# Seven of 39 expert slots cut from 256 rows to 128 in a mixture-of-experts layer

## The chip, the core and the metric

The kernel runs on one core of one Trainium2 chip. TensorE (PE) does the matrix products, VectorE (DVE) and ScalarE (ACT) the elementwise work, GpSimd (POOL) the indirect transfers, and SyncE (SP) issues the other transfers. The metric is the device time of one execution in microseconds (us): the median over several.

## The reference, cut to what matters

Two layers act on 4096 tokens of 256 numbers (x is 16 x 256 x 256). The change lies in the last part, the expert layer:

```python
shared = new_gelu(xf @ Wfc_s + bfc_s) @ Wproj_s + bproj_s
probs = softmax(xf @ Wr)                       # 8 experts
topk_p, topk_i = top_k(probs, 2); topk_p = topk_p / sum(topk_p)
gate[token, topk_i] += topk_p
for e in range(8):
    h = new_gelu(xf @ Wfc[e] + bfc[e]) @ Wproj[e] + bproj[e]     # 256 -> 1024 -> 256
    routed = routed + h * gate[:, e:e+1]
out = shared + routed
```

Each token needs two experts only, so 8192 rows (token, expert) are to be computed. How many fall to an expert is known only on the chip.

## The kernel before, in words

Attention, a quantised feed-forward layer and a Fourier stage come first and are not touched. The function `moe` normalises the tokens, runs the shared expert over 16 chunks of 256 tokens, and beside it VectorE works out the routing: `picks`, `slots_of_experts`, `slot_tables` (L2174: how many slots each expert takes, where they start, which expert each slot has), `row_ends` and `positions` (L2194: the place of each row). Then GpSimd sends each token's row to its two places in a table in memory, `slots_x`, by 64 indirect transfers (L1858).

The table is cut into slots of 256 rows; each slot belongs to one expert. An expert with n rows takes n/256 slots, rounded up, so at most (8192 + 8 x 255)/256 = 39 slots can be needed, and the program always works through 39; places without a token hold zeros and the number of no token. A slot is one round of `tick(s)`, which each engine runs in its own order:

- PE (L2049): `rows_T(s+1)` turns the next slot's rows (4 matmuls of 128x128, L1989); `first(s)` makes the hidden layer: 48 matmuls (8 column blocks x 2 halves of the input x 3 products of high and low parts), whose moving operand is the slot's 256 rows (L2004); `second(s-1)` makes the output of the slot before: for each 128 rows 24 matmuls whose moving operand is 256 weight columns (L2017).
- ACT: `copy_rows(s+1)` (L1912), `gelu(s)` (L1928).
- DVE: `low_rows(s+1)` (L2231), `shares(s+1)`, `cut(s)` into high and low half precision parts (L2135, L2137), `output(s-1)` (L2245, L2250).
- SP, one queue in this order: `slot_rows(s+2)` (L1812), `first_weights(s+2)` (L1797, 1 MB, waits for `gelu(s)`), `second_weights(s+1)` (L1804, 1 MB, waits until `output(s-1)` has read the products).
- POOL: `own` (L1864) and `add_rows` (L1872): two indirect transfers for each slot that add 128 rows each onto the result in memory; those of a slot start when those of the slot before have landed.

Weights, rows and results have two buffers each, by the parity of the slot. `walk` (L1748) writes ticks 0 and 1 out, loops 18 times over two ticks, and writes out the last. SP's and POOL's programs are written out in full.

Of the kernel before, what the change touches and what calls it, by code (L numbers as in the profile page):

```python
# [18 lines left out]
P = 128  # L19
# [1612 lines left out]

def moe(nc, d, g, X, ident, banks, halves_dram, out):
# [6 lines left out]
    NSLOT = (PICKS * NT * P + NE * (SLOT - 1)) // SLOT  # L1640
# [9 lines left out]
    with ExitStack() as ctx:  # L1650
# [6 lines left out]
        slots_x = nc.dram_tensor("slots_x", [NSLOT * SLOT, W], F32).ap()  # L1657
# [14 lines left out]
        e_table = sb("e_table", [P, NE, MOST])  # L1672
        s_table = sb("s_table", [P, NSLOT, NE])
# [12 lines left out]
        cmp_e = sb("cmp_e", [P, NE, MOST])  # L1686
        n_slots = sb("n_slots", [P, NE])
        start = sb("start", [P, NE + 1])
        cmp_s = sb("cmp_s", [P, NSLOT, NE])
        slot_ef = sb("slot_ef", [P, NSLOT])  # L1690
# [57 lines left out]
        def walk(eng, tick):  # L1748

            for s in range(2):  # L1750
                tick(s, s)
            with eng.Fori(1, NSLOT // 2) as i:
                for p in range(2):
                    tick(2 * i + p, p)
            for s in range(2 * (NSLOT // 2), NSLOT + 1):
                tick(s, s % 2)
# [5 lines left out]
        assert CHUNKS % 2 == 0 and NSLOT % 2 == 1  # L1762
# [11 lines left out]
        def _(sp):  # L1774
# [11 lines left out]
            n = NSLOT * SLOT // P  # L1786
# [3 lines left out]
            def expert(s):  # L1790
                return sp.value_load(slot_e[0:1, bass.ts(s, 1)], min_val=0, max_val=NE - 1)

            def first_weights(s, p):
                e = expert(s)
# [5 lines left out]
            def second_weights(s, p):  # L1800
                e = expert(s)
# [5 lines left out]
            def slot_rows(s, p):  # L1807
# [4 lines left out]
                sp.dma_start(rows[p][:], slots_x[bass.ts(s, SLOT), :].rearrange("(t p) c -> p t c", p=P)).then_inc(e_r[p], 16)  # L1812
# [12 lines left out]
            slot_rows(1, 1)  # L1825
            for c in range(CHUNKS - 4, CHUNKS):
                store_shared(c)
            first_weights(1, 1)
            second_weights(1, 1)

            def tick(s, p):
                if not (known(s) and s + 2 >= NSLOT):
                    slot_rows(s + 2, p)
                    first_weights(s + 2, p)
                if not (known(s) and (s < 1 or s + 1 >= NSLOT)):
                    second_weights(s + 1, 1 - p)

            for s in range(NSLOT + 1):
                tick(s, s % 2)

        @block.gpsimd
        def _(pool):
# [18 lines left out]
            def own(s):  # L1861
                p = s % 2
                pool.wait_ge(e_r[p], 8 * (s - p) + 16)
                pool.tensor_copy(owner[:, s, :], rows[p][:, :, TOKEN].bitcast(I32)).then_inc(e_own, 1)  # L1864

            def add_rows(s):
                pool.wait_ge(e_gt, s + 1)
                pool.wait_ge(e_own, s + 1)
                if s >= 1:
                    pool.wait_ge(e_sa, 16 * ST * s)  # L1870
                for t in range(ST):
# [11 lines left out]
            pool.wait_ge(e_sa, 16 * ST * NSLOT)  # L1883

        @block.scalar
        def _(act):
# [21 lines left out]
            def copy_rows(s, p):  # L1908
# [3 lines left out]
                act.activation(rT[p][:, 0, :, :].rearrange("p k t -> p (k t)"), banks[3][:, 512:1024], ACT.Copy).then_inc(e_rh, 1)  # L1912

            def gelu(n, p, buffer, ahead=()):
                ahead = list(ahead)
                for jp in range(J // 2):
# [8 lines left out]
                    for q in range(2):  # L1925
                        j = 2 * jp + q
                        src = banks[jp // 2][:, (jp % 2) * 512 + q * SLOT:(jp % 2) * 512 + (q + 1) * SLOT]
                        ins = act.activation(hf[p][:, j, :], src, ACT.Gelu_apprx_tanh, bias=b1[buffer][:, j:j + 1], scale=1.0 / WSCALE)  # L1928
# [22 lines left out]
            def tick(s, p):  # L1951
                if not (known(s) and s + 1 >= NSLOT):
                    copy_rows(s + 1, 1 - p)
# [424 lines left out]
```

## Time and profile before

| | us |
|---|---|
| median of 3 runs | 1328.8 (1327.67 to 1331.16) |
| the profiled execution | 1334.27 |
| its span, first to last instruction | 1332.5 |
| PE busy | 1170.6 (88%) |
| DVE busy | 851.9 (64%) |
| mean granted TensorE clock | 0.964 of full |

The span is read in stages: the shared expert from about 660 us to 870, the scatter of rows from 788 to 884, and the 39 slots from 887 to the end.

### The profile page before, as it was taken

What the parts mean: (1) busy time and instruction counts of PE and PEld (TensorE: products, weight loads), DVE (VectorE), ACT (ScalarE), POOL (GpSimd) and SP (SyncE); (2) the same over time, 40 slices, a digit from 0 to 9 for tenths busy, and PEclk for the clock granted to TensorE, in tenths of its full rate; (3) what the DMA queues carried; (4) which work ended last, traced back from release to release, by engine and by line L of the source; (5) the groups of instructions that cost most, each with busy time, mean ns of one, the idle gap of its engine ahead of it and who ended that gap; (6) DMA issues with size and microseconds to landing.
All of it is one profiled execution on the core that took longest, in us unless ns stands there. A gap on an engine that the chain in (4) does not pass through costs nothing. (4 is left out here: it accounts for less than half of the span.)

```text
span 1332.5 us, 28452 instructions
## 1 busy us (share of the span) xinstructions
PE 1170.6 (88%) x10152; PEld 891.3 (67%) x10152; DVE 851.9 (64%) x2620; ACT 595.4 (45%) x1065; POOL 587.4 (44%) x651
## 2 busy tenths in 40 slices
PE   0699999998678989975789999939999999999996
PEld 0144444444324668864679888828899999999995
DVE  3999999987796722255564785525666666666663
ACT  1388778777436612242075433313333333333331
POOL 6487787785610078952000026632333333333333
PEclk9999999999798999988979999969999999999999
DMA  9488879883500046502294043256888887888881
GB/s 277 86 169 167 173 170 168 176 184 103 190 2 1 1 142 213 181 32 73 82 262 102 1 164 107 99 177 213 256 253 252 252 252 241 248 250 247 252 256 50
DMA packets 183549, 217.30 MB, mean 163 GB/s; under 512 B 92944, under 2 KB 166288, under 8 KB 170912
## 3 DMA queue, kind: packets, MB, share of 16 engines
q1 hardware_dynamic: 169152, 199.19, 52.4%
q0 software_dynamic: 14304, 16.93, 6.1%
q8 instruction: 51, 0.84, 0.3%
q14 instruction: 42, 0.34, 0.1%
HBM read 144.70 MB, written 52.23 MB: 148 GB/s over the span
## 5 line engine op out<-in xcount | busy, mean ns | idle before, releaser
L2017 PE MATMUL banks<-moe_w,moe_hT 128*128 128x256 f16 x2640 | 296.9, 273 | 0.0
L2017 PEld LDWEIGHTS banks<-moe_w,moe_hT 128*128 128x128 f16 x2640 | 258.4, 98 | 30.0
L1928 ACT ACTIVATE moe_hf<-banks,moe_b 128x256 f32<-128x256 f32 x440 | 184.9, 471 | 171.0 <-PE banks L2004 171.0
L1872 POOL DMA_INDIRECT out_x<-moe_y,slot_owner x78 | 122.3, 1568 | 287.3 <-DVE moe_y L2250 238.2
L2004 PE MATMUL banks<-moe_rT,moe_w 128*128 128x256 f16 x1872 | 213.2, 274 | 0.0
L747 DVE CUSTOM_DVE_ANT_0 masked<-banks,mask_bias 128x256 f32<-128x256 f32 x512 | 185.9, 420 | 32.5 <-PE banks L569 28.6
L2004 PEld LDWEIGHTS banks<-moe_rT,moe_w 128*128 128x128 f16 x1872 | 184.6, 99 | 22.0
L2137 DVE TENSOR_TENSOR moe_hT<-moe_hf,moe_hT 128x512 f16<-128x512 f32 x220 | 153.9, 699 | 7.6
L479 ACT ACTIVATE probsT<-banks 128x1024 f32<-128x1024 f32 x128 | 130.7, 1021 | 50.4 <-PE banks L600 50.4
L569 PE MATMUL banks<-kT,qT 48*128 48x256 f16 x512 | 92.3, 285 | 50.8 <-DMA qT<-q_split 31.4
L1858 POOL DMA_INDIRECT slots_x<-moe_xn,pos x64 | 62.8, 981 | 155.1 <-DVE pos L2201 123.1
L2135 DVE CAST moe_hT<-moe_hf 128x512 f16<-128x512 f32 x220 | 95.4, 434 | 40.9 <-ACT moe_hf L1928 32.7
L1912 ACT ACTIVATE moe_rT<-banks 128x512 f16<-128x512 f32 x39 | 23.3, 597 | 209.8 <-PE banks L1989 209.8
L151 POOL TENSOR_SCALAR half_rows<-half_rows 128x512 f32<-128x512 f32 x72 | 108.1, 1502 | 10.9 <-issue 5.5
L2245 DVE SCALAR_TENSOR_TENSOR moe_y<-banks,moe_b 128x512 f32<-128x512 f32 x39 | 27.0, 692 | 133.5 <-PE banks L2017 133.5
L569 PEld LDWEIGHTS banks<-kT,qT 48*128 48x128 f16 x512 | 34.2, 95 | 108.7 <-issue 57.6
L2004 PE MATMUL banks<-moe_xnT,moe_w 128*128 128x256 f16 x768 | 91.3, 277 | 0.0
L155 POOL TENSOR_TENSOR half_parts<-half_rows,half_parts 128x512 f16<-128x512 f32 x72 | 84.8, 1178 | 6.2
L582 PE MATMUL banks<-qmT,kT 64*128 64x256 f16 x512 | 85.8, 278 | 0.0
L2004 PEld LDWEIGHTS banks<-moe_xnT,moe_w 128*128 128x128 f16 x768 | 76.4, 100 | 9.5
L1085 PE MATMUL banks<-xqT,w1T 128*128 128x512 bf16 x256 | 67.8, 395 | 12.5 <-ACT hf L1044 5.7
L615 PE MATMUL banks<-probsT,v_ones 128*32 128x256 f32 x1024 | 69.9, 392 | 0.3 <-ACT qmT L486 0.3
(322 smaller groups left out, 1783.4 us busy)
## 6 DMA issues: line engine op xcount, KB each, us to landing
moe_w<-moe_halves SPq DMA_DIRECT2D x80, 1024.0 KB, 5.0
moe_halves<-half_parts SPq DMA_DIRECT2D x18, 1024.0 KB, 6.1
slots_x<-empty_row SPq DMA_DIRECT2D x1, 10140.0 KB, 50.9
moe_rows<-slots_x SPq DMA_DIRECT2D x39, 260.0 KB, 5.9
half_rows<-in_L_ffn_Wfc SPq DMA_DIRECT2D x8, 1024.0 KB, 8.6
half_rows<-in_L_ffn_Wproj SPq DMA_DIRECT2D x8, 1024.0 KB, 8.5
moe_b<-in_L_ffn_bproj SPq DMA_DIRECT2D x39, 128.0 KB, 5.4
ctx_rows<-in_ctx SPq DMA_DIRECT2D x16, 256.0 KB, 3.0
```

Of the source, the lines that this page charges most:

```text
L151: pool.tensor_scalar(rows[:, cols], rows[:, cols], WSCALE, None, ALU.mult).then_inc(w["cut"], 1)
L155: pool.tensor_tensor(parts[:, 1, cols], rows[:, cols], parts[:, 0, cols], ALU.subtract).then_inc(w["cut"], 1)
L479: act.activation(probsT[n % EXPS][:].rearrange("p j k q -> p (j k q)"), psum_t[n % 2][:], ACT.Exp, scale=SCALE).then_inc(s_exp, 1)
L569: ins = pe.matmul(psum_s[:, at:at + S], qT[b % 2][rows, hp, t * P:(t + 1) * P], kT[b % 3][rows, hp, :], start=(t == 0), stop=(t == NQ - 1))
L582: pe.matmul(psum_t[n % 2][:, at:at + S], kT[b % 3][rows, hp, k * P:(k + 1) * P], qmT[b % 2][rows, hp, :], start=(k == 0), stop=False)
L747: ins = v.tensor_tensor_reduce(masked[2 * j + t][:], psum_s[:, at:at + S], mask_bias[b % 2][:, t, :], 1.0 / SHIFT, -3e38, ALU.add, ALU.max ...
L1872: pool.indirect_dma_start(out=out_rows, out_offset=bass.IndirectOffsetOnAxis(ap=owner[:, s, t:t + 1], axis=0), in_=y[s % 2][:, t, :], in_o ...
L1928: ins = act.activation(hf[p][:, j, :], src, ACT.Gelu_apprx_tanh, bias=b1[buffer][:, j:j + 1], scale=1.0 / WSCALE)
L2004: ins = pe.matmul(banks[jp // 2][:, at:at + SLOT], w1[buffer][:, w, k, j * P:(j + 1) * P], moving(x, k), start=(k == 0 and (w, x) == PARTS ...
L2017: ins = pe.matmul(OUT[p][:, t * D:(t + 1) * D], hT[p][:, x, j, t * P:(t + 1) * P], w2[buffer][:, w, j, :], start=(j == 0 and (w, x) == PAR ...
L2135: v.tensor_copy(hT[p][:, 0, at, :], hf[p][:, at, :]).then_inc(e_hh, 1)
L2137: v.tensor_tensor(hT[p][:, 1, at, :], hf[p][:, at, :], hT[p][:, 0, at, :], ALU.subtract).then_inc(e_hl, 1)
```

## The change

The 39 slots become 32 of 256 rows ("whole") and 7 of 128 ("half"). Rounds 2, 8, 14, 20, 26, 32 and 38 work on a half slot, the others on a whole one. In `slots_x` the whole slots lie first and the halves behind them, 71 tiles of 128 rows in place of 78. An expert's rows fill whole slots, and its last rows go to a half slot if there are at most 128 of them; if more whole slots are wanted than there are, a pair of halves is used as a whole one. So `slot_tables` counts both kinds, and `positions` moves the rows that lie in a half. `tick` takes the loop's number and the place in a period of six rounds; `walk` now writes out 6 ticks, loops 5 times over 6, and writes out the last 4.

```diff
+    halves = (2 * rows + NE * (SLOT - 2)) // SLOT
+    few = NE - 1
+    return (halves - few) // 2 + few, few, (halves - few) // 2
...
-            for s in range(2):
-                tick(s, s)
-            with eng.Fori(1, NSLOT // 2) as i:
-                for p in range(2):
-                    tick(2 * i + p, p)
+            for r in range(PERIOD):
+                tick(0, r)
+            with eng.Fori(1, NSLOT // PERIOD) as i:
+                for r in range(PERIOD):
+                    tick(i, r)
...
+        def tiles(r):
+            return 1 if r % PERIOD == HALF_AT else ST
...
-                for t in range(ST):
+                for t in range(tiles(s)):
                     pool.indirect_dma_start(out=out_rows, ...
...
-                ins = pe.matmul(banks[jp // 2][:, at:at + SLOT], w1[buffer][:, w, k, j * P:(j + 1) * P], moving(x, k),
+                ins = pe.matmul(banks[jp // 2][:, at:at + width], w1[buffer][:, w, k, j * P:(j + 1) * P], moving(x, k),
...
-                for t in range(ST):
+                for t in range(parts):
                     for j in range(J):
...
+                link(v.tensor_scalar(spill[:], start[:, NE, 0:1], -float(WHOLES), 0.0, ALU.add, ALU.max))
+                link(v.tensor_tensor(half_start[:], start[:, 0:NE, 1], start[:, 0:NE, 0], ALU.subtract))
...
+                link(v.tensor_tensor(tmp[:], base[:], over(whole_rows[:], full, 1), ALU.is_ge))
+                link(v.tensor_tensor(tmp[:], tmp[:], over(half_move[:], full, 1), ALU.mult))
                 link(v.scalar_tensor_tensor(base[:], over(start[:, 0:NE, 0], full, 1), float(SLOT), base[:], ALU.mult, ALU.add))
+                link(v.tensor_tensor(base[:], base[:], tmp[:], ALU.add))
```

On PE, in the last rounds of the program (behind the loop), the kernel before has the hidden layer of slot 38 and the outputs of slots 37 and 38; `moe_hT` is the hidden layer, `moe_w_0` and `moe_w_1` the weight buffers:

```order
L1752 COMPARE_AND_BRANCH
L2004 MATMUL banks<-moe_rT,moe_w_0 128x256 x48
L2017 MATMUL banks<-moe_w_1,moe_hT 128x256 x48
L2017 MATMUL banks<-moe_w_0,moe_hT 128x256 x48
L1650 UNCONDITIONAL_BRANCH
```

The changed kernel has slots 36, 37 and 38 there, of which 38 is a half:

```order
L1767 COMPARE_AND_BRANCH
L2027 MATMUL banks<-ident,moe_rows 128x128 x4
L2042 MATMUL banks<-moe_rT,moe_w_0 128x256 x48
L2055 MATMUL banks<-moe_w_1,moe_hT 128x256 x48
L2027 MATMUL banks<-ident,moe_rows 128x128 x2
L2042 MATMUL banks<-moe_rT,moe_w_1 128x256 x48
L2055 MATMUL banks<-moe_w_0,moe_hT 128x256 x48
L2042 MATMUL banks<-moe_rT,moe_w_0 128x128 x48
L2055 MATMUL banks<-moe_w_1,moe_hT 128x256 x48
L2055 MATMUL banks<-moe_w_0,moe_hT 128x256 x24
L1660 UNCONDITIONAL_BRANCH
```

A half slot keeps its 48 matmuls in the hidden layer, with 128 columns in place of 256, has 24 in place of 48 in the output, and 2 turns in place of 4. Its two weight transfers stay whole.

On VectorE the slot tables of the changed kernel read so; the names are those of the tables, `start` the running count of slots:

```order
L2218 TENSOR_TENSOR start<-start,n_slots 128x2 x8
L2219 TENSOR_SCALAR spill<-start 128x1
L2220 TENSOR_TENSOR half_start<-start 128x8
L2221 SCALAR_TENSOR_TENSOR half_start<-spill,half_start 128x8
L2222 TENSOR_TENSOR cmp_s<-s_table,start 128x312
L2223 TENSOR_TENSOR cmp_s<-s_table,half_start 128x56
L2224 TENSOR_REDUCE slot_ef<-cmp_s 128x46
L2225 SCALAR_TENSOR_TENSOR slot_ef<-cmp_s,slot_ef 128x7
L2226 TENSOR_TENSOR slot_ef<-slot_ef 128x7
L2227 TENSOR_SCALAR slot_rank<-slot_ef 128x39
L2228 TENSOR_SCALAR slot_e<-slot_ef 128x39
L2229 TENSOR_SCALAR whole_rows<-n_slots 128x8
```

Before, `start` was followed by one comparison, one sum and the two last conversions; the rest of these rows, and four more of 8 columns behind them, are new.

## Rows read from the trace of the kernel before

**Rows 1.** Page, the chain that ended last: share of the span
```profile
PE 38%; POOL 4%; DMA 3%; issue 2%; DVE 2%; SPq 0%; ACT 0%; POOLq 0%; DVEq 0%
```

**Rows 2.** Busy time by stretch: us, busy (instructions), PEclk, DMA share, GB/s
```profile
core 0: us, PE busy (x) PEld busy (x) DVE busy (x) ACT busy (x) POOL busy (x), PEclk, DMA share, GB/s
950.00:1300.00 350.00, 350.00 (x3209) 315.16 (x3207) 216.57 (x450) 127.16 (x290) 116.24 (x97) 1.00 0.83 251
```

**Rows 3.** Chain in order of time, one slot: start, us, what
```profile
1076.25 0.44 PE banks L1989 x4
1076.68 5.24 PE banks L2004 x48
1081.92 5.24 PE banks L2017 x48
```

**Rows 4.** Timeline of PE, 128-column matmuls with their own weights: start, us
```profile
338.54 1.07 PE L1060 MATMUL banks<-ident_bf,w1q_rounded 128*128 128x128 bf16 x16 [2.41 <-POOL pick_bias L988]
339.45 1.06 PE L1060 MATMUL banks<-ident_bf,w2q_rounded 128*128 128x128 bf16 x16
```

**Rows 5.** Timeline, end of the program
```profile
1316.01 0.69 DVE L2245 SCALAR_TENSOR_TENSOR moe_y<-banks,moe_b 128x512 f32<-128x512 f32 x1 [3.21 <-PE banks L2017]
...
1318.13 1.54 POOL L1872 DMA_INDIRECT out_x<-moe_y,slot_owner  x1 [6.54 <-DVE moe_y L2250]
...
1323.51 1.54 POOL L1872 DMA_INDIRECT out_x<-moe_y,slot_owner  x1 [1.99 <-DMA out_x<-moe_y,slot_owner]
1325.36 1.54 POOL L1872 DMA_INDIRECT out_x<-moe_y,slot_owner  x1 [0.30 <-issue]
```

**Rows 6.** Timeline, routing on VectorE and start of the scatter
```profile
772.40 1.52 DVE L2179 TENSOR_TENSOR start<-start,n_slots 128x1 f32<-128x1 f32 x8
...
775.30 0.42 DVE L2135 CAST moe_hT<-moe_hf 128x512 f16<-128x512 f32 x1
...
780.78 0.69 DVE L2142 SCALAR_TENSOR_TENSOR X<-banks,X 128x512 f32<-128x512 f32 x1 [1.15 <-PE banks L2017]
...
783.51 0.42 DVE L2195 TENSOR_TENSOR moe_base<-moe_base,tot 128x256 f32<-128x256 f32 x1
783.96 0.43 DVE L2196 TENSOR_TENSOR moe_base<-moe_base,moe_total 128x256 f32<-128x256 f32 x1
...
787.88 1.22 POOL L1858 DMA_INDIRECT slots_x<-moe_xn,pos  x1 [123.09 <-DVE pos L2201]
```

**Rows 7.** Timeline of SP's queue, one slot
```profile
1077.39 0.34 SPq L1804 DMA_DIRECT2D moe_w<-moe_halves  x1
1077.91 0.33 SPq L1805 DMA_DIRECT2D moe_b<-in_L_ffn_bproj  x1
1078.36 0.38 SPq L1812 DMA_DIRECT2D moe_rows<-slots_x  x1
1082.98 0.34 SPq L1797 DMA_DIRECT2D moe_w<-moe_halves  x1
```

**Rows 8.** The tile moe_rows: issue to landing
```profile
DMA to landing us min/median/max: 2.8/5.9/8.1
```

**Rows 9.** Busy time by stretch, around the end of a weight transfer
```profile
1087.50:1088.00 0.50, 0.50 (x7) 0.44 (x6) 0.50 (x1) 0.28 (x1) 0.00 (x0) 1.00 1.02 390
1088.50:1089.00 0.50, 0.50 (x7) 0.44 (x6) 0.50 (x3) 0.00 (x0) 0.00 (x0) 1.00 0.11 34
```

**Rows 10.** Timeline of PE, where the second slot starts
```profile
899.69 1.05 PE L1989 MATMUL banks<-ident,moe_rows 128*128 128x128 f32 x4 [2.52 <-DMA moe_rows<-slots_x]
```

**Rows 11.** Busy time by stretch, behind that wait
```profile
900.00:902.00 2.00, 2.00 (x11) 1.53 (x10) 0.59 (x1) 0.60 (x1) 0.00 (x0) 0.50 0.91 366
```

**Rows 12.** Chain in order of time, the hidden layer behind that wait
```profile
900.74 6.51 PE banks L2004 x48
```

**Rows 13.** Page, DMA queues: instruction packets of the whole program
```profile
q8 instruction: 51, 0.84, 0.3%
```

**Rows 14.** DMA queues from 950 to 1300 us: the only instruction packets
```profile
q14 instruction: 6, 0.05, 0.0%
```

More of the change, by code:

```diff
@@ L1748, in walk, with slot, tiles_before, place @@
         def walk(eng, tick):
-            for s in range(2):
-                tick(s, s)
-            with eng.Fori(1, NSLOT // 2) as i:
-                for p in range(2):
-                    tick(2 * i + p, p)
-            for s in range(2 * (NSLOT // 2), NSLOT + 1):
-                tick(s, s % 2)
+            for r in range(PERIOD):
[3 more added lines that the diff above has]
+                    tick(i, r)
+            for r in range(NSLOT % PERIOD + 1):
+                tick(NSLOT // PERIOD, r)
+        def slot(i, r):
+            return PERIOD * i + r
+        def tiles(r):
+            return 1 if r % PERIOD == HALF_AT else ST
+        def tiles_before(i, r):
+            whole, r = divmod(r, PERIOD)
+            return (ST * PERIOD - 1) * (i + whole) + sum(tiles(x) for x in range(r))
+        def place(i, r):
+            whole, r = divmod(r, PERIOD)
+            if r == HALF_AT:
+                return WHOLES + i + whole
+            return (PERIOD - 1) * (i + whole) + r - (r > HALF_AT)
+        def first_tile(i, r):
+            whole, q = divmod(r, PERIOD)
+            if q == HALF_AT:
+                return ST * WHOLES + i + whole
+            return ST * place(i, r)
         def known(s):
@@ L1798, in first_weights, with second_weights @@
                 sp.dma_start(b1[p][:], d["moe_b1"][bass.ds(e, 1)].rearrange("o p j -> p (o j)")).then_inc(e_w1[p], 16)
-            def second_weights(s, p):
-                e = expert(s)
+            def second_weights(i, r):
+                s, p, e = slot(i, r), r % 2, expert(i, r)
                 if not (known(s) and s == 0):
@@ L1824, in _ @@
             slot_rows(0, 0)
-            slot_rows(1, 1)
+            slot_rows(0, 1)
             for c in range(CHUNKS - 4, CHUNKS):
                 store_shared(c)
[L1828 to L1839, printed above, removed]
+            first_weights(0, 1)
+            second_weights(0, 1)
+            for s in range(NSLOT - 1):
+                if s + 2 < NSLOT:
+                    slot_rows(*divmod(s + 2, PERIOD))
+                    first_weights(*divmod(s + 2, PERIOD))
+                if s >= 1:
+                    second_weights(*divmod(s + 1, PERIOD))
         @block.gpsimd
@@ L2237, in shares @@
+            def shares(i, r):
+                s, p, n = slot(i, r), r % 2, tiles(r)
+                mine = share[:, bass.ds(ST * s, n)]
+                v.scalar_tensor_tensor(mine, rows[p][:, 0:n, RANK], slot_rank[:, bass.ts(place(i, r), 1)], rows[p][:, 0:n, EXTRA], ALU.is_equal, ALU.mult).then_inc(e_shr, 1)
                 v.wait_ge(e_shr, 2 * s + 1)
-                v.tensor_tensor(mine, mine, rows[p][:, :, GATE], ALU.add).then_inc(e_shr, 1)
-            def output(s, p):
+                v.tensor_tensor(mine, mine, rows[p][:, 0:n, GATE], ALU.add).then_inc(e_shr, 1)
@@ L2257, in tick @@
                 if not (known(s) and s >= NSLOT):
-                    cut(CHUNKS + s, p)
+                    cut(CHUNKS + s, p, width=tiles(r) * P)
                 if not (known(s) and s < 1):
-                    output(s - 1, 1 - p)
+                    output(i, r - 1)
             low_rows(0, 0)
@@ L2339, in routing_tables @@
     SLOT = 256
-    nslot = (2 * tokens + NE * (SLOT - 1)) // SLOT
+    nslot, halves, wholes = slot_counts(2 * tokens, NE)
+    full = np.arange(tokens // SLOT) * SLOT
+    both = np.concatenate([full + SLOT // 2, full])
+    order = np.concatenate([np.arange(wholes), wholes + np.arange(halves) // 2, np.arange(halves)])
     f = np.float32
```

152 lines of the change are left out of this document (88 added, 64 removed).

## The prediction

> **What bounds the kernel now.** I read first the page's chain of waits: PE holds 38% of what ended last, POOL 4% and the DMAs 3% [rows 1]. The rest of the chain is not named there, since it lies in stages that the change doesn't touch. Then the busy time by stretch: from 950 to 1300 us PE is busy for 350.00 of 350 us, at the full clock (2.4 GHz), while DVE has 217 us, ACT 127 and POOL 116, and the DMA engines are busy 0.83 of the time at 251 GB/s [rows 2]. So in the slots PE alone sets the time, and the DMA is the one other resource that is not far from its limit. The chain there is a plain repetition: 0.44 us of turns, 5.24 us of `first`, 5.24 us of `second`, 10.92 us for each slot of 256 rows [rows 3]. That is 109.2 ns for each matmul of 256 columns.
>
> **The change part by part.**
>
> *Hidden layer of a half slot.* 48 matmuls of 128 columns in place of 256. The trace has such matmuls elsewhere, each with weights of its own: 16 take 339.45 - 338.54 = 0.91 us from start to start, 57 ns each [rows 4]; a little of that is the group's first, so I take 56. Saved: 48 x (109.2 - 56) = 2.55 us for each half, 7 x 2.55 = 17.9 us.
>
> The Trainium skill ("TensorE: Matmul & The Clock Gate", Back-to-back issue gap) says that in a stream of weight loads and matmuls the spacing at 128 columns is about 81 ns, since both share the pipeline. By it the hidden layer of a half would give 48 x 28.2 = 1.35 us, 9.5 us in all. The 57 ns of the row are for just such pairs and speak against it; it is a rival below.
>
> *Output of a half slot.* 24 matmuls of 256 columns go: 24 x 109.2 = 2.62 us, 18.3 us for seven. *Turns.* 2 of 4 go, 0.22 us, 1.5 us for seven. PE's sum is 37.7 us.
>
> *The end.* The output of the last slot is on another path. The product of slot 37 is ready at 1316.0, its additions start at 1318.1, and those of slot 38 wait until they have landed at 1323.5 [rows 5]. That wait doesn't shrink with slot 38's 2.62 us on PE. What goes is the second of its two additions, 1325.36 - 1323.51 = 1.85 us. So 0.8 us of the sum is given back.
>
> *Routing on VectorE.* The slot tables get 11 more instructions on 1 to 56 columns, and three grow. The eight small ones of before take 1.55 us from start to start, 0.19 each [rows 6]; 11 x 0.2 is 2.2, and the wider ones add some 0.3: 2.5 us. Behind them stands the cutting of a chunk, which starts at 775.30; behind it DVE waits 1.15 us for PE, until 780.78 [rows 6]. So 1.15 us of the 2.5 is hidden and 1.35 is late. `positions` gets three instructions of 256 columns at 783.96 - 783.51 = 0.45 us [rows 6], 1.35 us, all in the open: the scatter waits for it and for nothing else (POOL idle for 123 us until `pos`). The scatter starts 2.7 us later, and so do the slots. PE doesn't feel it earlier: `second` of that chunk comes one `first` (5.24 us) behind 780.8, at 786, and its cut, which ended 1.15 us before 780.78, now ends at 782.1. Bounds: 1.35 us (if the tables were hidden) and 4 us.
>
> *First slots.* PE waits 2.52 us for the rows of slot 2 [rows 10]. They are a half slot now; half of their bytes (130 KB) at 251 GB/s are 0.5 us less.
>
> *Transfers.* Each half still wants 2 MB of weights and 128 KB of bias, against half of the rows and of the additions. Over six rounds the bytes fall from 16.5 to some 16.1 MB while PE's time falls from 65.5 to 60.1 us: 268 GB/s, against 251 at 0.83 busy, which would be 302 at 1.0. On average it fits. What is tight is one transfer: the rows of slot s+2. SP issues them behind `second_weights`, 2.1 us after the round's start at 1076.25 [rows 3, 7], they land 5.9 us later (median) [rows 8], at 8.0 us, and PE wants them at the start of the next round, at 10.92. The slack is 2.9 us. A round with the half slot's `first` takes 0.44 + 2.69 + 5.24 = 8.37 us, and the round behind it, with its `second`, 0.44 + 5.24 + 2.62 = 8.30. In the first the rows come about 0.3 us early. In the second the queue is still full: `first_weights` is issued 2.55 us earlier in the short round, but moves only behind the rows, from 7.5 us on. A weight transfer takes about 4 us (1 MB at 251 GB/s), so it ends near 11.5 to 12, while the next `second_weights` would begin to move at about 10.7; before, the queue had run empty at that point (390 GB/s, then 34) [rows 9]. So these rows land about 1.3 us later than usual, at 9.3 against 8.30: PE waits 1.0 us. For six halves (none follows the seventh): 6.0 us. Bounds: 0 if the transfers are fast enough to keep the order, and 2.5 us each if the additions in memory, which run beside them, slow the weights further: 0 to 15 us. I take 6.0. The new waits stand in front of the turns on PE, so `first` and `second` of that round move with them; the transfers issued after them move as well, which gives the queue the time to empty. The other rounds have 2.9 us to spare.
>
> DVE and ACT follow: in the short round DVE has the output of a whole slot and the cut of half a slot, under 6 us of 8.4. POOL's additions of one slot take less than a full round, and a half has one in place of two.
>
> **The sum**: -17.9 - 18.3 - 1.5 + 0.8 + 2.7 - 0.5 + 6.0 = -28.7 us. It is made against the profiled execution (1334.27 us, 1.8 more than its span); that is 5.5 us over the median of the runs. The slots show no difference of that kind (rounds are equal to 0.01 us), so I take the sum from the median: 1328.8 - 28.7 = 1300.1 us.
>
> **The rivals.**
>
> *A, no new wait* (0 in place of 6.0): 1294 us. For it: the landing times scatter, and the median leaves 0.3 us of slack even in a short round. Against it: 0.83 busy before, and the same weights in less time.
>
> *B, the transfers are slower than I think*: 2.5 us for each half, 15 us: 1309 us. After a wait of 2.52 us the clock stood at 0.50 (1.2 GHz) and `first` took 6.51 us in place of 5.24, 1.3 more [rows 10 to 12]; if the new waits did that too, 1317. For it: the additions. Against it: the round in between gives the queue 2.6 us back.
>
> *C, the hidden layer of a half is bound by its weight loads*: as if each pair took 81 ns in place of 56, 25 x 336 = 8.4 us more: 1308.5 us; nothing less than the pace of [rows 4] has a row in this trace. For it: those rows are a burst of 32, not 48 beside other work.
>
> *D, the loop no longer keeps its instructions.* From 950 to 1300 us some 16 turns of the old loop show no packet of q8, the queue that brought 51 in the whole program [rows 13, 14]: a body of two ticks is not fetched again. The new body has six ticks, 574 matmuls in place of 200. If each of the four jumps back had to wait for a fetch, at 2.8 to 8.1 us as other small transfers land [rows 8], that is 11 to 32 us, partly under the matmuls that PE has queued: 1311 us with 2.8, more with 8.1. The Trainium skill ("Runtime: NRT & Kernel Launch", Instruction fetch mechanics) gives PE room for 2048 instructions and says that a jump out of the window forces a fetch; the new body has some 1200, so by the larger figure it fits, while the same section also speaks of two blocks only, by which it wouldn't. No run here shows which.
>
> *E, slower than before.* The rows of the two slots behind each half land behind a whole further weight transfer, and the clock falls each time. It takes 34.7 us (28.7 + 6.0) to use up the gain: 5.8 us for each of six halves, or 2.9 us at each of both rounds with 1.3 us of slow clock in it. At this point it is slower: from 1.6 us of pure wait plus the clock in both. At 4 us of weights and 1.3 of clock in both rounds it is 6 x 10.6 = 64 us: 1358. Against it: the queue keeps its order, and no weight transfer is issued between `second_weights` and the rows.
>
> **How the numbers follow.** Forecast 0.62, A 0.12, B 0.10, C 0.08, D 0.05, E 0.03. The time is that of the forecast, 1300.1. Its own range is 1296 to 1305; with A and C, and the smaller B, 1291 to 1310 holds a little over 8 in 10. What a measurement can tell from no change is about 0.3%, 4 us. Faster: all but E and the far ends of B and D, 0.96; the same 0.02; slower 0.02.
>
> **What the profile will show.** Right: rounds of a half at 2.7 us for 48 hidden matmuls and 2.62 for 24 output ones; the scatter's first transfer 2.7 us after its old place relative to the shared expert; waits of PE for `moe_rows` of about 1 us behind halves, none elsewhere; clock 1.00 from 950 us on. Wrong: hidden matmuls of a half at 3.9 us (C), packets of the instruction queue and idle PE at every sixth round (D), waits of over 2 us with clock 0.50 behind them (B, E), or no waits at all (A).

## The result, and the profile after

The changed kernel takes 1304.8 us (1304.07 to 1307.15, four runs) against 1328.8 before: ratio 0.982, 95% interval 0.9801 to 0.9839. The forecast was 1300.1, a ratio of 0.9784. Two further measurements, on two other chips, gave 0.9796 (0.9761 to 0.9832) and 0.9772 (0.9744 to 0.9800). So the forecast lies inside two of the three intervals, and a little under the first one.

The profiled execution took 1305.47 us, its span is 1303.7. The page's chain and the busy time by stretch, in the columns of [rows 1, 2]:

```profile
PE 31%; DMA 6%; POOL 4%; DVE 3%; issue 2%; ACT 1%; SPq 1%; DVEq 0%; POOLq 0%
```

```profile
950.00:1270.00 320.00, 316.08 (x2999) 284.06 (x2998) 196.23 (x430) 117.10 (x279) 103.16 (x88) 1.00 0.87 265
```

PE's share of the chain fell from 38 to 31%, the DMAs' rose from 3 to 6%: PE is no longer without a gap in the slots, and the bytes per second rose from 251 to 265. Where PE stands still, and for what, is read from the chain in order of time (start, us, what), over both short rounds of one half slot:

```profile
974.44 0.44 PE banks L2027 x4
974.88 2.68 PE banks L2042 x48
977.56 5.25 PE banks L2055 x48
...
983.03 0.70 DVE moe_y L2301
...
983.92 0.34 SPq L1841
...
984.89 7.66 DMA moe_rows<-slots_x
...
992.67 0.65 PE banks L2027 x4
```

The half slot shown has the longest wait of the six that can have one. The 48 hidden matmuls of a half take 2.68 us, 55.8 ns each. The round behind it ends in rows that were issued at 984.89 and landed 7.66 us later. Where the chain runs through `moe_rows`, the rows set the time and not PE. PE's own timeline over the same two rounds (start, us, ..., idle before it and what ended that):

```profile
977.39 5.40 PE L2055 MATMUL banks<-moe_w,moe_hT 128*128 128x256 f16 x48
983.93 0.66 PE L2027 MATMUL banks<-ident,moe_rows 128*128 128x128 f32 x4 [1.13 <-DMA moe_rows<-slots_x]
...
989.66 2.78 PE L2055 MATMUL banks<-moe_w,moe_hT 128*128 128x256 f16 x24
992.67 0.65 PE L2027 MATMUL banks<-ident,moe_rows 128*128 128x128 f32 x4 [0.23 <-DMA moe_rows<-slots_x]
```

I count a wait from start to start: 48 matmuls of 109.2 ns from 977.39 on end at 982.63, and the turns come at 983.93, 1.30 us later; in the second round it is 0.39. (The idle time in the brackets is less by the 0.16 us that a matmul's modelled end reaches over the next start.)

SP's queue in the first of these rounds (start, us), to be read beside [rows 7]:

```profile
975.58 0.34 SPq L1841 DMA_DIRECT2D moe_w<-moe_halves  x1
...
976.55 0.38 SPq L1850 DMA_DIRECT2D moe_rows<-slots_x  x1
978.40 0.34 SPq L1834 DMA_DIRECT2D moe_w<-moe_halves  x1
```

The rows are issued 2.1 us into the round, as before. But the next `first_weights` (L1834) now follows them by 1.85 us, where it was 4.62 [rows 7]: its wait is for the half's hidden layer, and that is 2.55 us shorter. The rows land at 983.88, 7.33 us after their issue. Over the six half rounds of this trace the median is 6.6 us, where the same six rounds of before have 6.0.

Whether the weights move beside the rows can be counted. Weights go in packets of 8 KB, rows in packets of 1040 bytes. So here are all packets between the first and the last one of the rows: in this round, in the next half round (1043.06 to 1044.58 us) and in the same round of before (1049.84 to 1051.32 us). Those that are not under 8 KB are weights.

```profile
DMA packets 390, 0.90 MB, mean 329 GB/s; under 512 B 31, under 2 KB 317, under 8 KB 317
```

```profile
DMA packets 368, 0.37 MB, mean 241 GB/s; under 512 B 28, under 2 KB 366, under 8 KB 366
```

```profile
DMA packets 425, 0.41 MB, mean 274 GB/s; under 512 B 33, under 2 KB 425, under 8 KB 425
```

In the round shown above 73 of the 128 weight packets of a transfer run beside the rows; in the next half round it is 2, and before the change none. The same count over the 18 half rounds of the three traces of the changed kernel gives two kinds. In 5 of them 44 to 88 packets run beside the rows, and TensorE waits 1.0 to 1.8 us; in the other 13 it is 23 packets or fewer, the first packet of the rows only starts some 0.5 us later than before, and TensorE waits 0.3 to 0.8 us. What holds the first packet back there is not shown. Nor is what makes the other kind; in all 5 of them POOL's additions start late, 3.1 to 6.0 us into the round, against 2.4 to 2.8 in 12 of the 13.

The routing and the start of the scatter, in the columns of [rows 6]: first the sum of chunk 5 before the change, then the changed kernel:

```profile
770.30 0.69 DVE L2142 SCALAR_TENSOR_TENSOR X<-banks,X 128x512 f32<-128x512 f32 x1 [1.37 <-PE banks L2017]
```

```profile
767.43 0.69 DVE L2181 SCALAR_TENSOR_TENSOR X<-banks,X 128x512 f32<-128x512 f32 x1 [1.38 <-PE banks L2055]
...
779.17 0.68 DVE L2181 SCALAR_TENSOR_TENSOR X<-banks,X 128x512 f32<-128x512 f32 x1
...
787.65 1.21 POOL L1893 DMA_INDIRECT slots_x<-moe_xn,pos  x1 [125.50 <-DVE pos L2254]
```

The idle 1.15 us in front of the sum is gone, as the prediction had it. In the trace of before, the sum of chunk 5 (L2142) stands at 770.30 and the scatter starts at 787.88 [rows 6], 17.58 us later; here it is 787.65 - 767.43 = 20.22. The difference is 2.64 us. That the absolute times are nearly the same is because this execution was 2.87 us ahead when it reached the tables.

### The profile page after: what moved, and what is told of

It reads as the page before. It is cut to its first block and busy times, and to the rows that moved or that the text cites. A ratio compares the mean times of both kernels' runs of the same rounds, so it can differ in the third digit from the quotient of the medians.

```text
span 1303.7 us, 27826 instructions
## 1 busy us (share of the span) xinstructions
PE 1135.0 (87%) x9970; PEld 858.2 (66%) x9970; DVE 836.4 (64%) x2627; ACT 587.0 (45%) x1065; POOL 575.2 (44%) x644
## 5 line engine op out<-in xcount | busy, mean ns | idle before, releaser
L2055 PE MATMUL banks<-moe_w,moe_hT 128*128 128x256 f16 x2472 | 278.5, 273 | 0.0
L2055 PEld LDWEIGHTS banks<-moe_w,moe_hT 128*128 128x128 f16 x2472 | 241.6, 98 | 27.9
L1964 ACT ACTIVATE moe_hf<-banks,moe_b 128x256 f32<-128x256 f32 (+1 forms) x440 | 178.5, 457 | 158.7 <-PE banks L2042 157.7
L1907 POOL DMA_INDIRECT out_x<-moe_y,slot_owner x71 | 116.1, 1636 | 268.5 <-DMA out_x<-moe_y,slot_owner 138.6
L2042 PE MATMUL banks<-moe_rT,moe_w 128*128 128x256 f16 (+1 forms) x1872 | 194.0, 264 | 0.0
L2042 PEld LDWEIGHTS banks<-moe_rT,moe_w 128*128 128x128 f16 x1872 | 170.3, 98 | 17.7
L2176 DVE TENSOR_TENSOR moe_hT<-moe_hf,moe_hT 128x512 f16<-128x512 f32 (+1 forms) x220 | 145.6, 662 | 7.6
L2174 DVE CAST moe_hT<-moe_hf 128x512 f16<-128x512 f32 (+1 forms) x220 | 91.8, 417 | 45.6 <-ACT moe_hf L1964 42.9
L1948 ACT ACTIVATE moe_rT<-banks 128x512 f16<-128x512 f32 (+1 forms) x39 | 21.8, 559 | 205.2 <-PE banks L2027 205.2
L2301 DVE SCALAR_TENSOR_TENSOR moe_y<-banks,moe_b 128x512 f32<-128x512 f32 (+1 forms) x39 | 25.1, 644 | 112.3 <-PE banks L2055 101.5
L1085 PE MATMUL banks<-xqT,w1T 128*128 128x512 bf16 x256 | 68.5, 398 | 11.8 <-DVE hidden_max L1206 5.4
```

The costliest lines, as they stand in the source:

```text
L1907: pool.indirect_dma_start(out=out_rows, out_offset=bass.IndirectOffsetOnAxis(ap=owner[:, s, t:t + 1], axis=0), in_=y[s % 2][:, t, :], in_o ...
L1964: ins = act.activation(hf[p][:, j, 0:width], src, ACT.Gelu_apprx_tanh, bias=b1[buffer][:, j:j + 1], scale=1.0 / WSCALE)
L2042: ins = pe.matmul(banks[jp // 2][:, at:at + width], w1[buffer][:, w, k, j * P:(j + 1) * P], moving(x, k), start=(k == 0 and (w, x) == PART ...
L2055: ins = pe.matmul(OUT[p][:, t * D:(t + 1) * D], hT[p][:, x, j, t * P:(t + 1) * P], w2[buffer][:, w, j, :], start=(j == 0 and (w, x) == PAR ...
L2174: v.tensor_copy(hT[p][:, 0, at, 0:width], hf[p][:, at, 0:width]).then_inc(e_hh, 1)
L2176: v.tensor_tensor(hT[p][:, 1, at, 0:width], hf[p][:, at, 0:width], hT[p][:, 0, at, 0:width], ALU.subtract).then_inc(e_hl, 1)
```

## The experiments

One trace of each kernel wasn't enough here, so the first thing to read is a table over all of them. The program has four stages around the change: from the sum of chunk 5 on VectorE to the scatter's first transfer (routing), from its first to its last issue (scatter), from there to the first turn of slot 0 (start), and from that turn to the end of the span (slots). Times in us, worked out from the starts of these instructions in each trace.

| kernel | routing | scatter | start | slots | ratio to before, 95% interval |
|---|---|---|---|---|---|
| before, two traces | 17.6, 17.6 | 93.9, 93.5 | 5.4, 5.3 | 445.4, 445.5 | 1 |
| changed, three traces | 20.2 each | 97.8, 93.6, 97.7 | 5.4, 6.6, 5.5 | 412.9, 417.4, 413.1 | 0.982; 0.9796; 0.9772 (above) |
| before with the routing's extra work | 20.2 | 96.1 | 5.3 | 443.2 | 1.0023 (1.0008 to 1.0038) |
| changed, TensorE at full width | 20.2 | 92.7 | 10.5 | 441.8 | 1.0013 (0.9998 to 1.0028) |
| changed, hidden at full width | 20.2 | 96.2 | 5.5 | 424.3 | 0.9912 (0.989 to 0.9934) |
| changed, output at full width | 20.2 | 93.9 | 5.4 | 427.0 | 0.986 (0.9835 to 0.9886) |
| changed, plain writes | 20.2 | 96.1 | 5.4 | 423.0 | one run, 1319.05 us |
| rows early, two traces | 20.2 each | 94.6, 95.1 | 5.3, 5.4 | 406.1, 407.0 | 0.9762 (0.9737 to 0.9787); 0.9724 (0.9696 to 0.9753) |
| rows and positions early, two traces | 14.6 each | 93.6, 96.4 | 9.7, 5.5 | 410.0, 405.4 | 0.9727 (0.9704 to 0.975); 0.9691 (0.9662 to 0.972) |

The column on the right compares many runs, the others are single executions. Routing is the same to 0.05 us in all traces with the same program on VectorE; the scatter is not. Nor are the slots: with the code of before they took 445.4, 445.5 and, in the experiment on the routing, 443.2 us, since the wait for the rows of slot 2 was 2.5, 3.0 and 1.1 us, and the hidden layer behind it took 6.6, 6.9 and 5.2.

**The routing alone**, in the kernel before:

```diff
+                for _ in range(12):
+                    link(v.tensor_scalar(spare[:], n_slots[:], 2.0, None, ALU.mult))
...
                 link(v.scalar_tensor_tensor(base[:], over(start[:, 0:NE], full, 1), float(SLOT), base[:], ...
+                for _ in range(3):
+                    link(v.tensor_tensor(tmp[:], base[:], over(spare[:], full, 1), ALU.mult))
```

> The kernel before with 12 small instructions added to VectorE's slot tables (tensor_scalar on 7 columns, 0.2 us each) and 3 of 256 columns in positions (0.45 us each); what they compute is not used. Theory (the prediction's step): 1.35 us of the first group is hidden behind VectorE's wait of 1.15 us, the rest stands ahead of the scatter: the scatter starts 2.6 us later, the scatter itself takes 96 us as before, 1328.8 + 2.6 = 1331.4 us. Rival: all of it is hidden (the scatter has another releaser): 1328.8. Second rival, for the 4.0 us that the changed kernel's scatter took longer (100.35 against 96.33 us from start to the rows' issue): it comes with the later start, by what runs beside the scatter then: 1331.4 + 4 = 1335.4, scatter at 100 us here as well.

Measured: ratio 1.0023, 3.1 us (1.1 to 5.1). VectorE and POOL in its trace:

```profile
766.68 0.69 DVE L2143 SCALAR_TENSOR_TENSOR X<-banks,X 128x512 f32<-128x512 f32 x1 [1.37 <-PE banks L2018]
...
786.88 1.22 POOL L1859 DMA_INDIRECT slots_x<-moe_xn,pos  x1 [126.40 <-DVE pos L2206]
```

20.20 us in place of 17.58: the extra instructions cost 2.6 us and none of it is hidden but the 1.15 us of the wait. The step of the sum holds. The scatter took 96.1 us here, in the old layout.

**TensorE at full width for the half slots.**

```diff
-                    first(CHUNKS + s, p, lambda x, k: rT[p][:, x, k, 0:n], width=n)
+                    first(CHUNKS + s, p, lambda x, k: rT[p][:, x, k, :])
...
-                    second(CHUNKS + s - 1, 1 - p, 1 - p, tiles(r - 1))
+                    second(CHUNKS + s - 1, 1 - p, 1 - p)
```

> The changed kernel, but TensorE does the half slots at full width: 48 hidden matmuls of 256 columns (the upper 128 are left over from another slot and not used) and 48 output matmuls. All else of the change stays. Theory: what is left beside TensorE's saving is turns -1.5, the first wait for rows -2.3 (as the changed kernel's trace shows: 1.49 us idle and no slow clock, in place of 2.52 and 1.3), the last slot's second addition -1.9, the routing +2.7, no wait for rows at half slots: 1328.8 - 3.0 = 1325.8 us. If the scatter's extra 4.0 us is an effect of the new layout and no chance of one profile: 1329.8 us, with 100 us of scatter in this trace too. Rival: the waits for rows stay with rounds of 10.9 us (the queue, not the short round, makes them): 6 us more than either.

Measured: ratio 1.0013, 1.7 us slower than before where 3.0 us faster was expected. The expectation missed. The slots took 441.8 us, 3.6 less than before, and the routing costs 2.6 more: that leaves 1.0 us faster. Of the 5.7 us that the slots were to lose, 2.1 didn't come: most of it is the wait for the rows of slot 2, 3.57 us here, with 6.91 us for the hidden layer behind it. The trace adds a loss of its own, 10.5 us from the last issue of the scatter to the first turn in place of 5.4: here TensorE ended the shared expert only at 890.8, later than the scatter (more on it below). Waits for rows behind slot 2: none. Whether these two account for the other runs too isn't known, since one was traced. What it shows for certain is that without TensorE's shorter rounds the change gains nothing.

**Only the hidden layer at full width** (the first of the two edits above).

> The changed kernel, but the hidden layer of a half slot runs at 256 columns (upper 128 left over, not used); its output stays at 24 matmuls. Theory: +17.9 us on TensorE, and the waits for rows at the end of the half's own round (3.7 us in six) go, since that round is 10.8 us again; those of the second round (2.4 us) stay: 1304.8 + 17.9 - 3.7 = 1319.0 us. Rival: the waits are set by the bytes that the queue has to move over both rounds and not by the length of one: they stay at 6 us, 1322.7 us, or all of them go, 1316.6.

Measured: ratio 0.9912, or 1317.1 us on the scale of the 1328.8 (1314.2 to 1320.1, which excludes 1322.7 and can't tell 1319.0 from 1316.6; the trace can). The slots took 11.4 us more than in the first trace of the changed kernel, which is the second rival's 17.9 - 6.1 = 11.8: all the waits go, those of the second round too (0.6 us of idle in five places is left). SP's queue in this trace:

```profile
976.29 0.38 SPq L1850 DMA_DIRECT2D moe_rows<-slots_x  x1
980.70 0.34 SPq L1834 DMA_DIRECT2D moe_w<-moe_halves  x1
```

The weights are again 4.4 us behind the rows. In the half's own round a wait could hardly arise, since it lasts 10.9 us again; but the rows land sooner too, 5.9 us behind their issue (median of the six, 5.8 to 5.9) against 6.6 in the changed kernel, and no weight packet moves beside them. The round behind is as short as in the changed kernel, 8.30 us, and there they take 6.0 us against 7.1. So it is the short hidden layer that makes the rows late in both rounds; in its own round the earlier issue of the weights behind them is the only difference in SP's queue.

**Only the output at full width** (the second edit).

> The changed kernel, but the output of a half slot runs 48 matmuls (the second half of the rows is left over from another slot and not used); its hidden layer stays at 128 columns. Theory: both waits of a half come from the round with the short hidden layer, in which the rows of slot h+2 are issued at the usual time but wanted 2.55 us earlier; the wait at its end (3.7 us in six) stays, and the one a round later (2.4 us) goes, since that round is 10.9 us again; with +18.3 of outputs and -0.8 at the end: 1304.8 + 17.5 - 2.4 = 1319.9 us. Rival: the wait of the second round is handed on from the first (a late transfer makes the next ones late) and stays: 1322.3 us.

Measured: ratio 0.986, or 1310.2 us (1306.9 to 1314.2) where 1319.9 or 1322.3 was expected: as a time both missed. The changed kernel measured beside it was at 0.9796 and not at the 0.982 from which they were worked out, and its trace, with 8.9 us of waits for rows, has only 9.6 us less in the slots. Against the first trace, the slots took 14.1 us more, not 15.1. Of this, the sum in the expectation was wrong at one place: the output of the last slot isn't on the path at all, since its addition waits for those of the slot before. With it full, the span ends 10.2 us behind the last matmul and not 12.8, and the end doesn't move. So 18.3 - 2.6 - 2.4 = 13.3 was to be expected. The waits for rows:

```profile
PE banks L2027 <- DMA moe_rows<-slots_x: 3.7, 7, 1.5
```

From start to start they come to 4.8 us: six of them, 4.2 us, are at the end of the half's own round, none is at the end of the next, and one of 0.6 us is at a whole round elsewhere. For the places of the waits the theory holds: the round with the short hidden layer makes a wait by itself, the one with the short output only behind it.

**The rows issued early.** The waits for rows in the changed kernel, and this edit against them:

```profile
PE banks L2027 <- DMA moe_rows<-slots_x: 4.4, 9, 1.1
```

```diff
+            slot_rows(0, 2)
             for s in range(NSLOT - 1):
+                if s + 3 < NSLOT:
+                    slot_rows(*divmod(s + 3, PERIOD))
                 if s + 2 < NSLOT:
-                    slot_rows(*divmod(s + 2, PERIOD))
                     first_weights(*divmod(s + 2, PERIOD))
```

> The changed kernel, but SyncE issues the rows of slot s+3 ahead of first_weights(s+2) and second_weights(s+1), a weight pair earlier than before. Theory (the rows come late because they stand behind second_weights in the queue): TensorE's waits for rows at half slots, 6.1 us in twelve, go, and nothing takes their place, since the weights have slack: 1304.8 - 6.1 = 1298.7 us. Rival (the DMA's bandwidth is the limit in the short rounds): the weights are late in place of the rows, by as much: 1304.8 us, with waits for moe_w in the trace.

> The rows issued early, again, beside the changed kernel: no wait for rows from slot 3 on, and 6 to 9 us less than the changed kernel (ratio between the two 0.993 to 0.995). Rival: only the 2 to 3 us that the early scatter gave it last time are real beyond the waits of one trace: 0.997.

Measured: 0.9762 and, beside a changed kernel at 0.9772 on the same chip, 0.9724: 0.995 of it, 6.4 us less, at the lower end of the 6 to 9 expected. The slots took 406.1 and 407.0 us against 412.9 to 417.4. The chain of the second of these traces, over both short rounds:

```profile
912.14 0.44 PE banks L2029 x4
912.57 2.68 PE banks L2044 x48
915.25 5.24 PE banks L2057 x48
920.49 0.44 PE banks L2029 x4
920.93 5.24 PE banks L2044 x48
926.17 2.62 PE banks L2057 x24
928.79 0.44 PE banks L2029 x4
```

```profile
950.00:1270.00 320.00, 320.00 (x3051) 289.52 (x3050) 202.03 (x443) 121.04 (x288) 109.08 (x91) 1.00 0.89 268
```

The rounds are 8.35 and 8.30 us and PE has no gap, at 268 GB/s and a share of 0.89. No wait for weights took the place of that for rows. So the DMAs were fast enough for the short rounds; the place of the rows in SP's queue, behind a pair of weight transfers, was what cost the 6 to 9 us of waits.

**The changed kernel and the kernel before once more**, unchanged.

> The changed kernel once more, for the 4.7 us between 1300.1 and the measured 1304.8. Theory: the steps from the first slot on are as predicted, and the miss lies in the scatter, whose length differs from execution to execution (92.7 to 97.8 us from its first to its last issue in the six traces so far, with no order by kernel): with more runs the ratio to the kernel before goes from 0.982 towards 0.979, and this trace has a scatter between those ends. Rival: the ratio stays at 0.982 and the scatter at 97 us or more: the new layout costs the scatter 4 us.

> The kernel before once more, for one more trace of it. Theory: its scatter too lies anywhere between 92.5 and 98 us from first to last issue, and the time from the start of the program to the slot tables differs by some us from 770.3. Rival: 93.9 us again and 770.3 again, which would make these properties of the kernel.

> The changed kernel a third time, in the same batch as the two corrected kernels. Theory: TensorE's waits for the rows at half slots differ from execution to execution (6.1 and 8.9 us in the two traces so far), and so do the scatter and the end of the shared expert; the ratio lies between the 0.982 and the 0.980 measured so far. Rival: one of them is an outlier, and the ratio is that of the forecast, 0.978, with waits of 6 us or less.

Measured: 0.9796 and 0.9772 for the changed kernel, where the first measurement had 0.982. Its scatter took 97.8, 93.6 and 97.7 us; the eleven traces with the new layout lie between 92.7 and 97.8 (mean 95.2), the three with the old one between 93.5 and 96.1 (mean 94.5). The rival, that the layout costs the scatter 4 us, has no support; 1 us isn't excluded by so few traces. The expectation that the third measurement would lie between the other two missed: it came out lower, at 0.977. The waits for rows, from start to start, were 6.1, 8.9 and 6.3 us (one, three and one round with many weight packets beside the rows):

```profile
PE banks L2027 <- DMA moe_rows<-slots_x: 7.1, 10, 1.6
```

This line is the second trace by the view that groups waits, to be compared with the 4.4 of the first. The time to the tables differs as well: the sum of chunk 5 stands at 767.6 in the repeat of before and at 770.3 in the first trace. So neither number belongs to a kernel.

**Rows and positions early.** On VectorE, on top of the early rows:

```diff
+            row_ends()
+            positions()
             cut(7, 1)
             shared_output(6, 0)
-            row_ends()
-            positions()
```

> The kernel with the rows issued early, and on VectorE row_ends and positions ahead of the cutting of chunk 7 and the sum of chunk 6 in place of behind them. Theory: the scatter is waited for alone (TensorE idles 5 to 23 us ahead of the first slot), so its start, 5.6 us earlier (4.3 of cutting and 1.3 of sums that it no longer waits for), moves the end by as much: 5.6 us less than with the rows early alone, ratio to before 0.972. Rival: TensorE, which then waits 2 us for chunk 7, is late with the shared expert and becomes the bound: 0.976 as with the rows early alone, or up to 2 us more.

> Rows early and positions early, beside the rows early alone. Theory after its first trace, where TensorE ended the shared expert at 889 us, later than the scatter: the start of the scatter is worth its 5.6 us only where TensorE is done by then, so the gain over rows early alone is between 0 and 5.6 us, about 3: ratio to the kernel before 0.973. Rival: it was hidden by chance, and the full 5.6 come now: 0.971.

Measured: 0.9727 and 0.9691, beside 0.9762 and 0.9724 of the early rows alone: 4.7 and 4.4 us less in the middle, with intervals of 3 to 4 us on each side (the first two on different chips, the second two on one). This fits the 5.6 us and isn't told apart from 3; the theory of the second expectation, 0.973, lies above its interval, and its rival, 0.971, inside. The scatter's start behind the sum of chunk 5, in the second trace:

```profile
769.94 0.69 DVE L2183 SCALAR_TENSOR_TENSOR X<-banks,X 128x512 f32<-128x512 f32 x1 [1.38 <-PE banks L2057]
...
784.57 1.22 POOL L1895 DMA_INDIRECT slots_x<-moe_xn,pos  x1 [120.55 <-DVE pos L2256]
```

14.6 us in place of 20.2. In the first trace 4.4 us of this was lost again, since TensorE ended the shared expert later than the rows came, as the first expectation's rival had it, and some 4 us more at the start of slot 2 (a wait of 4.49 us, and 7.78 for the hidden layer behind it); in the second it waited 1.98 us for them and nothing was lost. This is the fastest version of the study, and faster than both kernels.

**Plain writes in place of additions.**

```diff
-                                            in_=y[s % 2][:, t, :], in_offset=None, bounds_check=NT * P - 1, oob_is_err=False,
-                                            compute_op=ALU.add).then_inc(e_sa, 16)
+                                            in_=y[s % 2][:, t, :], in_offset=None, bounds_check=NT * P - 1, oob_is_err=False).then_inc(e_sa, 16)
```

> The changed kernel, but the slots' rows are written to the output and not added to it: the same bytes to the same places without reading the sum there, so the output lacks the other terms. Theory: the rows of slot h+2 are late since they stand behind second_weights in the queue, whatever the additions do: TensorE's waits at half slots stay at 6 to 9 us; at the end of the program the last transfers land sooner, some 2 to 4 us. Rival (the additions slow the queue, as the forecast's case B had it): the waits fall under 3 us.

Measured: 1319.05 us in a single run, the slots 423.0. Neither theory has it: the waits grew, to 13.8 us from start to start. By the view that groups waits, from 908 us on (behind slot 2, as in the lines above):

```profile
PE banks L2026 <- DMA moe_rows<-slots_x: 11.8, 12, 2.0
```

The software queue's packets, MB and share of the 16 engines, in the changed kernel from 950 to 1270 us and then in this one:

```profile
q0 software_dynamic: 8358, 6.94, 15.8%
```

```profile
q0 software_dynamic: 2736, 6.80, 5.4%
```

The additions take three times the engine time of writes for about the same bytes, and yet taking that away doesn't let the rows land sooner. In the half's own rounds the waits are 4.2 us in six, against 3.7, 6.1 and 4.4 in the three traces of the changed kernel: there the additions aren't what makes the rows late, and for these rounds case B's reason, that the additions slow the queue, has no support. All of the growth is in the second rounds, 9.6 us against 2.4, 2.2 and 2.0. There the plain writes don't stand where the additions stood. In all six second rounds POOL issues them 1.7 to 3.1 and 3.0 to 4.5 us into the round, where the additions of the three traces come at 4.7 to 6.3 and 6.5 to 7.7. So all of their bytes move while the rows move, and with them 37 to 103 weight packets, against 4 to 45 in the three traces. These are the packets between the first and the last one of the rows in the second round of slot 8: in the changed kernel (988.72 to 992.05 us) and here (994.97 to 999.69 us).

```profile
DMA packets 501, 0.71 MB, mean 214 GB/s; under 512 B 42, under 2 KB 469, under 8 KB 469
...
q0 software_dynamic: 67, 0.07, 24.9%
```

```profile
DMA packets 620, 1.50 MB, mean 317 GB/s; under 512 B 77, under 2 KB 453, under 8 KB 517
...
q0 software_dynamic: 96, 0.26, 13.9%
```

The weight packets are 32 in the one and 103 in the other. So this edit changed when the transfers run as well as what they cost, and for the second rounds it doesn't test case B alone. Why the rows take so long there isn't settled. Nor did the end gain the 2 to 4 us: 12.8 us from the last matmul as before.

## Why the prediction was right

By the steps of the sum, stage by stage. The traces give -31.0 us for the slots (mean of 412.9, 417.4 and 413.1 against 445.45) and +2.6 for the routing, -28.4 together, where the sum had -28.7. With two and three traces, and slots that differ by 4.5 us in one and the same kernel, this agrees better than it could be known to.

- *Hidden layer, -17.9*: 2.68 us for 48 matmuls, in every round of the chain; saved 2.56 each. Right, and case C (3.9 us) is out. The Trainium skill ("TensorE: Matmul & The Clock Gate", Back-to-back issue gap) gives 81 ns for a pair at 128 columns; this trace has 55.8.
- *Output, -18.3, and +0.8 at the end*: 2.62 us for each half that another slot follows. For the last slot the step was put as 2.62 less 0.8; what the trace shows is that its matmuls give nothing and the second addition that went gives the gain. From the product of slot 37 to the end of the span it was 16.5 us (1316.01 to 1332.5, [rows 5]) and is 15.1 now (1288.57 to 1303.7), 1.4 us less where the step had 1.85. VectorE and POOL at the end of the changed kernel:

```profile
1288.57 0.69 DVE L2301 SCALAR_TENSOR_TENSOR moe_y<-banks,moe_b 128x512 f32<-128x512 f32 x1 [3.83 <-PE banks L2055]
...
1290.69 1.54 POOL L1907 DMA_INDIRECT out_x<-moe_y,slot_owner  x1 [4.47 <-DVE moe_y L2306]
...
1297.17 1.54 POOL L1907 DMA_INDIRECT out_x<-moe_y,slot_owner  x1 [3.10 <-DMA out_x<-moe_y,slot_owner]
```
- *Turns, -1.5*: 0.22 us less in each, right.
- *Routing, +2.7*: 2.64 us in the trace, 2.62 in the experiment of its own. Right.
- *First slots, -0.5*: undersized. PE waited 1.49 us for the rows of slot 2 in place of 2.52, and the clock stayed up: `first` behind it took 5.24 us, not 6.51 [rows 10 to 12]. That is 2.3 us in this trace. In the other traces of the new layout the same wait lies between nothing and 4.5 us, so it is no fixed gain.

```profile
902.38 0.44 PE banks L2027 x2
902.82 5.24 PE banks L2042 x48
```

- *Waits for rows, +6.0*: 6.1, 8.9 and 6.3 us, so the size was right or a little low, but that is luck: the reasoning had no wait in the first short round and 1.0 us in the second, 0 and 6.0 in all, and the three traces have 3.7, 6.1 and 4.4 us in the six first rounds and 2.4, 2.2 and 2.0 in the second ones (the second trace has 0.6 more one round later). Two steps failed, in opposite directions. The first is "In the first the rows come about 0.3 us early": it took their 5.9 us from issue to landing as unchanged, since `first_weights` "moves only behind the rows". It is issued 1.85 us behind them in this trace, and the rows land 6.6 us behind their issue (median), 0.5 us too late. In 13 of 18 such rounds the weights still follow the rows almost whole, and the rows start later; in 5 they move beside them, and the wait is 1.0 us or more. The second is the time in the next round: there the rows are under way for 7.1 us in place of 6.0, 1.2 more where 1.3 was put, but SP issues them some 0.5 us earlier in a round that itself began late, so PE waits 0.4 us and not 1.0. The experiment with the hidden layer at full width bears out both: the rows land as before in both rounds, and 0.6 us of waits is left.
- *Case D*: from 950 to 1300 us there are seven instruction packets of q8 now, where [rows 14] had none. Five of them come by 1012 us, while the loop's body is passed for the first time (952.7 to 1014.6), and two from 1270 on, behind the loop; from 1012 to 1268 us, over the four jumps back, there is none. So the body is not fetched again, and with the rows issued early PE is busy for 320.00 of 320 us, over the jumps. The loop costs nothing. The larger of the two figures in the Trainium skill ("Runtime: NRT & Kernel Launch", Instruction fetch mechanics), by which the body fits, agrees with that; the smaller doesn't.

From 952 to 1012 us:

```profile
q8 instruction: 5, 0.08, 0.5%
```

What lies between -28.4 and the measured -23.9, -27.1 and -30.3 (each ratio on 1328.8) is not in a step of the sum, and its place is open. The first pair of profiles doesn't show it: their spans differ by 28.8 us (-32.5 in the slots, +2.6 in the routing, +3.9 in the scatter, -2.9 ahead of the tables), while the medians of four runs differ by 24.0. The sum was read from an execution 5.5 us above its kernel's median, as the prediction says, and the changed kernel's profiled execution is only 0.7 above. Runs without a trace can't be divided by stage. What the traces do show is how much one execution can add: the scatter differs by 5 us with no order by layout, the slots of the changed kernel by 4.5. The range held all three.

## What to carry to other kernels

When a piece of work on the bounding engine is made shorter, look for the instructions of other queues that wait for its end: they come earlier too, and here a weight transfer that was issued 2.8 us earlier made the small transfer ahead of it land late, by 0.6 us in the median and by 1 us and more where the two ran side by side. If the next thing wanted stands behind something that isn't wanted yet, change the order of issue before you look for bandwidth: it took away 6 to 9 us of waits at an unchanged number of bytes. And take a second trace of the unchanged kernel before you explain a few us: in three traces of the changed kernel the routing was equal to 0.1 us, and the other stages moved by 1 to 5 us.

## What of the hardware was not expected

During the scatter TensorE often stands still for 0.2 to 0.9 us (once 1.7) with nothing that the profile shows to wait for, some 1.4 us apart, about as far as the scatter's transfers. The first traces of the two kernels have none of it; all twelve taken later, on three chips, the kernel before included, have 2.6 to 13.2 us of it in all. PE in one of them, the second trace of the changed kernel:

```profile
821.06 0.61 PE L2055 MATMUL banks<-moe_w,moe_hT 128*128 128x256 f16 x4 [0.44 <-issue]
822.50 0.70 PE L2055 MATMUL banks<-moe_w,moe_hT 128*128 128x256 f16 x3 [0.83 <-issue]
823.91 6.58 PE L2055 MATMUL banks<-moe_w,moe_hT 128*128 128x256 f16 x34 [0.71 <-issue]
```

The same 60 us of the kernel before, in its first trace and in its repeat, with the granted clock in the column PEclk:

```profile
800.00:860.00 60.00, 60.00 (x552) 53.77 (x551) 34.55 (x58) 19.94 (x48) 39.20 (x40) 1.00 0.30 105
```

```profile
800.00:860.00 60.00, 53.43 (x453) 44.30 (x452) 27.05 (x47) 14.76 (x38) 40.49 (x41) 0.97 0.30 108
```

In the first, the shared expert ended 17 us ahead of the first turn, and the scatter alone was waited for; in the repeat it ended 1.6 us ahead of it, and in three of the fourteen traces it was the later of the two. The lower clock costs as well. In the second trace of the changed kernel, shown above, TensorE stands still for 11.2 us in all, but the shared expert ends 21 us later behind the scatter's start than in the first; the granted clock was 1.00 from 790 to 860 us in the first, and 0.83 on average from 810 to 850 us in the second. What stops TensorE is open. For this kernel it means that the scatter can be shortened by a few us only before TensorE is the bound there.
